# A graph attention layer on one core: TensorE adds messages up before it makes z, and two of its three signals a quad go

## Chip, cores and metric

The kernel runs on one NeuronCore of a Trainium2 chip. The metric is the device time of one execution in microseconds (us); for the kernel before it was 2990.29 us, the median of three runs (2976.26 to 2995.08).

## What is computed

Two graph layers over 6250 nodes of 128 features and 106250 edges sorted by destination, each closed by a residual and a layer norm. The change is in the attention of the second (layer 1), which the reference computes so (cut):

```python
h = _layer_norm(x, ln1_w)
xl = (h @ lin_l_w.T + lin_l_b).reshape(n, h_heads, c)     # 8 heads of 16
xr = (h @ lin_r_w.T + lin_r_b).reshape(n, h_heads, c)
e = (edge_attr @ lin_edge_w.T).reshape(-1, h_heads, c)
z = jax.nn.leaky_relu(xl[src] + xr[dst] + e, NEG_SLOPE)
logits = jnp.einsum('ehc,hc->eh', z, att)
m = jax.lax.stop_gradient(jax.ops.segment_max(logits, dst, num_segments=n))
num = jnp.exp(logits - m[dst])
den = jax.ops.segment_sum(num, dst, num_segments=n)
alpha = num / den[dst]
msg = xl[src] * alpha[..., None]
attn_out = jax.ops.segment_sum(msg, dst, num_segments=n).reshape(n, d) + attn_bias
```

Everything is float32 here but some 0/1 flags.

## The kernel before

Edges are cut into tiles of 128, four tiles are a quad (512 edges), and four quads are a group. There are 52 groups, so 208 quads. The program has three stages, one after the other: layer 0, the attention of layer 1, and the MLP with the last norm. Only the second is touched. In it each engine has its own program, written out by hand, one step for each quad Q; semaphores alone tie the engines together, and each engine takes its instructions strictly in that order.

What each engine does for a quad:

- GpSimd (POOL) issues four indirect gathers that bring the rows of `xl` of the quad's sources (L846). For quad Q it waits for z of quad Q - 4 (`z_ready`).
- SyncE (SP) loads the windows of `xr` (L830), and once a group the edge attributes and the destination offsets (L828, L826). It waits for `z_ready` too.
- TensorE (PE), `make_z`: z in PSUM is the sum of the edge attributes times a weight (L905), the window of `xr` spread over the edges by a 0/1 matrix (L909), and the gathered rows turned (L913). The last of these signals `z_ready`. `make_logits` (L925) multiplies the activated z by the attention vector and signals `lg_ready`. `add_up` (L956) multiplies the messages by a 0/1 matrix, which gives each tile's sums per destination, and signals `summed`. Once a group come `sum_ends` (L935), `spread_shares` (L940, L941) and `turn_alpha` (L948), each with a signal of its own.
- ScalarE (ACT), `split_z` (L857, L858): the leaky relu as two activations out of z's PSUM buffer, of which there are two. `keep_shrunk` (L873) takes what L941 made, once a group.
- VectorE (DVE): `make_spread` (L991) makes the 0/1 matrix for z; `add_tile` (L1022), four times a quad, adds the tile sums into the node sums in SBUF; `send_messages` (L1000) and `make_onehots` (L1010) make both operands of `add_up`; in between stand the small steps of the softmax of a group, `find_run_max` (L1042), `pick_grown` (L1146, which waits for ACT's L873), `share_out` (L1140, for which L940 waits) and others.

The order in time: in step Q, PE makes z of quad Q + 1, the logits of quad Q and the sums of quad Q - 10. DVE in its step Q makes the spread matrix of quad Q + 1, adds the sums of quad Q - 11 and makes messages and 0/1 matrices of quad Q - 9. The constant `LAG` is 9. Buffers for spread, z, messages, 0/1 matrices and tile sums are doubled.

Of the kernel before, what the change touches and what calls it, by code (L numbers as in the profile page):

```python
# [29 lines left out]
QUADS = CHUNKS // QT  # L30
# [14 lines left out]
def build(nc, t, N, E):  # L45
# [40 lines left out]
    quads = tiles // QT  # L86
# [11 lines left out]
    with ExitStack() as ctx:  # L98
# [87 lines left out]
        summed = sem("summed")  # L186
# [508 lines left out]
    attention = ExitStack()  # L695
    LAG = 9
    ROWS = 16
    AHEAD = 4
    node_sums = attention.enter_context(nc.sbuf_tensor("node_sums1", [P, NP], F32))
    with ExitStack() as ctx:  # L700
# [81 lines left out]
        z_ready = sem("z_ready")  # L782
        z_split = sem("z_split")
        lg_ready = sem("lg_ready")
# [19 lines left out]
        summed = sem("summed1")  # L804
        added = sem("added1")
        attr_dram = t["attrT"]
        with nc.Block() as block:
# [43 lines left out]
            @block.scalar  # L851
            def _(act):
                def split_z(Q):
                    act.wait_ge(z_ready, Q + 1)
                    if Q >= 2:
                        act.wait_ge(lg_ready, Q - 1)
                    nc.scalar.activation(z_act[:, Q % 2, 0, :], z_ps[Q % 2][:], ACT.Identity, bias=z_bias[:, 0:1], scale=0.2)  # L857
                    nc.scalar.activation(z_act[:, Q % 2, 1, :], z_ps[Q % 2][:], ACT.Relu, bias=z_bias[:, 1:2],  # L858
                                         scale=0.8).then_inc(z_split, 1)

                def raise_power(s):
                    act.wait_ge(lowered, s + 1)
                    nc.scalar.activation(power[:], power[:], ACT.Exp).then_inc(powered, 1)

                def raise_falls(s):
                    act.wait_ge(falls_made, 2 * s + 2)
                    nc.scalar.activation(falls[:], falls[:], ACT.Exp).then_inc(fell, 1)

                def keep_shrunk(s):
                    act.wait_ge(shares_spread, s + 1)  # L870
                    if s >= 2:
                        act.wait_ge(added, (s - 1) * CHUNKS)
                    nc.scalar.copy(shrunk[:, s % 2], shares_ps).then_inc(shrunk_made, 1)  # L873

                def norm_x1(b):
                    for i in range(block_tiles(b)):
                        at = b * QT + i
                        nc.scalar.activation(x1[:, b, i, :], x1[:, b, i, :], ACT.Identity, bias=shift1[:, at:at + 1],
                                             scale=rstd1[:, at:at + 1])

                nc.scalar.activation(std1[:], mv1[:].rearrange("p b i m -> p (b i) m")[:, :, 1], ACT.Sqrt,
                                     bias=eps_cols[:, 0:1]).then_inc(std1_made, 1)
                act.wait_ge(shift1_made, 1)
                for Q in range(quads + LAG):
                    s = Q // QUADS - 1
                    if Q < quads:
                        split_z(Q)
                    if Q % QUADS == 0 and 0 <= s - 1 < groups:
                        keep_shrunk(s - 1)
                    if Q % QUADS == 0 and 0 <= s < groups:  # L890
                        raise_power(s)
                    if Q % QUADS == 2 and 0 <= s < groups:
                        raise_falls(s)
                    if Q >= LAG and Q - LAG < blocks:
                        norm_x1(Q - LAG)

            @block.tensor
            def _(pe):
# [18 lines left out]
                def make_logits(Q):  # L917
                    s, q = Q // QUADS, Q % QUADS
                    pe.wait_ge(z_split, Q + 1)
                    if q == 0 and s >= 2:  # L920
                        pe.wait_ge(lowered, s - 1)
                    for part in range(2):
                        for i in range(QT):
                            lanes = slice(i * 32, i * 32 + 32)
                            mm = nc.tensor.matmul(lg_ps[s % 2][lanes, 0, :], att_pad[:, q, :],  # L925
                                                  z_act[:, Q % 2, part, i * P:(i + 1) * P],
                                                  start=(q == 0 and part == 0), stop=(q == QUADS - 1 and part == 1),
                                                  tile_position=(0, i * 32))
                    mm.then_inc(lg_ready, 1)

                def sum_ends(s):
                    pe.wait_ge(ends_picked, 2 * s + 2)
# [11 lines left out]
                def turn_alpha(s):  # L944
                    pe.wait_ge(alpha_made, s + 1)
                    if s:
                        pe.wait_ge(message_made, s * QUADS)
                    nc.tensor.transpose(alpha_ps, alpha[:], ident[:]).then_inc(alpha_turned, 1)  # L948

                def add_up(Q):  # L950
                    pe.wait_ge(onehot_made, Q + 1)
                    pe.wait_ge(message_made, Q + 1)
                    if Q >= 2:
                        pe.wait_ge(added, (Q - 1) * QT)
                    for i in range(QT):
                        mm = nc.tensor.matmul(tile_sums[Q % 2][:, i, :], message[:, Q % 2, i, :], onehot[:, Q % 2, i, :],  # L956
                                              start=True, stop=True)
                    mm.then_inc(summed, 1)

                pe.wait_ge(masks_made, 3)  # L960
                nc.tensor.transpose(alpha_ps[:, 0:HEADS], head_lanes[:], ident[0:HEADS, 0:HEADS])
# [7 lines left out]
                for Q in range(quads + LAG + 1):  # L969
                    s = Q // QUADS - 1  # L970
                    if Q % QUADS == 2 and 0 <= s < groups:
                        sum_ends(s)
                    if Q % QUADS == 0 and 0 <= s - 1 < groups:
                        spread_shares(s - 1)
                    if Q % QUADS == 1 and 0 <= s - 1 < groups:
                        turn_alpha(s - 1)
                    if Q + 1 < quads:
                        make_z(Q + 1)
                    if Q < quads:
                        make_logits(Q)  # L980
                    if Q >= LAG + 1:
                        add_up(Q - LAG - 1)

            @block.vector
            def _(dve):
                def make_spread(Q):
                    s, at = Q // QUADS, Q % QUADS * QW
                    dve.wait_ge(rel_in[s % 2], (s // 2 + 1) * DMA)
                    if Q >= 2:
                        dve.wait_ge(z_ready, Q - 1)  # L990
                    nc.vector.tensor_scalar(spread[:, Q % 2, :], rel_bc[:, s % 2, at:at + QW], iota_col[:, 0:1], None,  # L991
                                            ALU.is_equal).then_inc(spread_made, 1)

                def send_messages(Q):
                    s, q = Q // QUADS, Q % QUADS
                    dve.wait_ge(alpha_turned, s + 1)
                    if Q >= 2:
                        dve.wait_ge(summed, Q - 1)
                    mine = alpha_ps.rearrange("p (k l) -> p k l", k=QT)[:, :, q * HEADS:(q + 1) * HEADS]
                    nc.vector.tensor_tensor(message[:, Q % 2].rearrange("p k (h c) -> p k h c", h=HEADS),  # L1000
                                            rows[:, Q % ROWS].rearrange("p k (h c) -> p k h c", h=HEADS),
                                            mine.unsqueeze(3).to_broadcast([P, QT, HEADS, HC]),
                                            ALU.mult).then_inc(message_made, 1)

                def make_onehots(Q):
                    if Q >= 2:
                        dve.wait_ge(summed, Q - 1)
                    for i in range(QT):
                        tile = Q * QT + i
                        o = nc.vector.tensor_scalar(onehot[:, Q % 2, i, :], iota_row[:], rel_cols[:, tile:tile + 1], None,  # L1010
                                                    ALU.is_equal)
                    o.then_inc(onehot_made, 1)

                def add_tile(Q, i, base):
                    tile = Q * QT + i
                    if i == 0:
                        dve.wait_ge(summed, Q + 1)
                        dve.wait_ge(shrunk_made, Q // QUADS + 1)
                    if tile:
                        dve.wait_ge(added, tile)  # L1020
                    span = node_sums[:, bass.ds(base, P)]
                    nc.vector.scalar_tensor_tensor(span, span, shrunk[:, Q // QUADS % 2, 1, tile % CHUNKS:tile % CHUNKS + 1],  # L1022
                                                   tile_sums[Q % 2][:, i, :], ALU.mult, ALU.add).then_inc(added, 1)
# [13 lines left out]
                                            ALU.mult).then_inc(fences_made, 1)  # L1037

                def find_run_max(s):
                    dve.wait_ge(lg_ready, (s + 1) * QUADS)  # L1040
                    dve.wait_ge(fences_made, s + 1)
                    nc.vector.tensor_tensor_scan(run_max[:], fence[:, s % 2, 0:P], lg_ps[s % 2][:, 0, :], -BIG, ALU.add,  # L1042
                                                 ALU.max).then_inc(segment_step, 1)
# [156 lines left out]
                for Q in range(quads + LAG + 2):  # L1200
                    s, q = Q // QUADS - 1, Q % QUADS
# [334 lines left out]
```

## Time and profile before

| | |
|---|---|
| median of three runs | 2990.29 us |
| the profiled execution | 2994.84 us, of which 2993.0 us are the span from the first to the last instruction |
| attention of layer 1 within the span | from about 1472 to 2870 us, 208 quads |
| TensorE granted clock over the span | 0.826 of full |
| busy over the span | PE 74%, DVE 57%, ACT 38%, POOL 58% |

Times below are from that one profiled execution. PE is TensorE's matmul row, PEld its weight loads. A bracket at a row's end says how long the engine stood idle ahead of it and which instruction's signal ended that; "remote" there means a semaphore's event that the reader of the trace could not tie to one instruction that had just ended, and "issue" that nothing in the profile explains the idle time.

### The profile page before, as it was taken

Reading aid. Unit: us, or ns where it says so; the run is one execution under the profiler, and the core shown is the slowest. Engines: PE = TensorE matmul, PEld = TensorE weight load, DVE = VectorE, ACT = ScalarE, POOL = GpSimd, SP = SyncE. Lnnn points to the kernel's source line nnn. Section 1 sums busy time; section 2 is a strip of 40 time slices with the busy share of each in tenths; the row PEclk is TensorE's granted clock in tenths of the full one; section 3 lists DMA queues with packets and bytes.
Section 4 is the critical chain, followed back from the end, with each engine's and each line's share of the span. In section 5 each row is a group of like instructions: output and inputs, shape, how many; then the busy total and the mean of one; then the engine's idle time right before and its main releaser. Section 6 shows DMA issues by size and latency. Waiting matters only on the chain. (4 is left out here: it accounts for less than half of the span.)

```text
span 2993.0 us, 52671 instructions
## 1 busy us (share of the span) xinstructions
PE 2201.2 (74%) x14461; PEld 1756.5 (59%) x14461; DVE 1718.3 (57%) x7092; ACT 1126.6 (38%) x2973; POOL 1725.0 (58%) x1739
## 2 busy tenths in 40 slices
PE   7766665666666666667578888887888887888779
PEld 5665665665555666556355555555555665656556
DVE  2355555555555555557346656666666666666766
ACT  2355555555555555555333222222222222222123
POOL 3356666666666666655565656666666666666322
PEclk9687788788788877887788888987888888888879
DMA  5344444444444444432644444444444444444201
GB/s 136 97 117 111 109 112 105 113 113 109 109 111 114 106 112 112 123 88 59 171 148 141 147 142 126 144 143 140 144 146 147 144 131 139 146 146 147 62 20 36
DMA packets 378501, 356.41 MB, mean 119 GB/s; under 512 B 61695, under 2 KB 335743, under 8 KB 371424
## 3 DMA queue, kind: packets, MB, share of 16 engines
q1 hardware_dynamic: 314640, 236.51, 28.3%
q0 software_dynamic: 53248, 109.16, 14.2%
q10 hardware_dynamic: 10320, 7.37, 0.9%
q8 instruction: 118, 1.93, 0.3%
q14 instruction: 175, 1.43, 0.2%
HBM read 338.98 MB, written 13.82 MB: 118 GB/s over the span
## 5 line engine op out<-in xcount | busy, mean ns | idle before, releaser
L846 POOL DMA_INDIRECT rows<-xl_tab,src_cols x832 | 844.0, 1014 | 505.9 <-issue 228.1
L279 POOL DMA_INDIRECT rows<-in_x,src_cols x832 | 796.6, 957 | 537.0 <-issue 208.9
L330 PE MATMUL tile_sums<-gather,rows 128*128 128x128 f32 x1664 | 420.1, 342 | 254.4 <-DVE node_sums L560 172.4
L560 DVE TENSOR_TENSOR node_sums<-node_sums,tile_sums 128x256 f32 x832 | 350.0, 421 | 387.1 <-PE tile_sums L332 182.9
L330 PEld LDWEIGHTS tile_sums<-gather,rows 128*128 128x128 f32 x1664 | 322.9, 241 | 296.7 <-issue 190.1
L320 PE MATMUL p_dst<-window,spread 128*128 128x129 f32 x1664 | 331.1, 333 | 200.9 <-issue 154.1
L1022 DVE SCALAR_TENSOR_TENSOR node_sums<-node_sums,shrunk,tile_sums 128x128 f32 x832 | 280.7, 337 | 238.2 <-remote 175.6
L320 PEld LDWEIGHTS p_dst<-window,spread 128*128 128x128 f32 x1664 | 283.6, 241 | 219.8 <-issue 207.6
L332 PE MATMUL tile_sums<-gather,ones 128*128 128x128 f32 x1664 | 389.8, 323 | 0.0
L548 DVE CUSTOM_DVE_ANT_0 product<-rows,p_dst 128x128 f32<-128x128 f32 x832 | 258.2, 348 | 226.3 <-remote 147.7
L909 PEld LDWEIGHTS z_ps<-spread,window 128*128 128x128 f32 x1664 | 254.6, 221 | 155.2 <-issue 132.9
L446 ACT ACTIVATE gather<-apart,weight,minus 128x128 f32<-128x128 bf16 x832 | 342.6, 482 | 7.0 <-issue 0.2
L332 PEld LDWEIGHTS tile_sums<-gather,ones 128*128 128x128 f32 x1664 | 322.3, 241 | 0.0
L956 PE MATMUL tile_sums<-onehot,message 128*128 128x128 f32 x1664 | 297.8, 327 | 30.7 <-issue 22.5
L857 ACT ACTIVATE z_act<-z_ps,z_bias 128x512 f32<-128x512 f32 x208 | 141.8, 682 | 456.0 <-remote 218.9
L925 PE MATMUL lg_ps<-z_act,att_pad 128*32 128x128 f32 x3328 | 212.3, 299 | 121.6 <-issue 117.4
L956 PEld LDWEIGHTS tile_sums<-onehot,message 128*128 128x128 f32 x1664 | 247.1, 225 | 88.2 <-issue 75.2
L905 PE MATMUL z_ps<-attr,w_e 128*128 128x512 f32 x416 | 272.5, 740 | 12.7 <-issue 12.3
L909 PE MATMUL z_ps<-spread,window 128*128 128x128 f32 x1664 | 262.0, 307 | 13.8 <-issue 11.4
L432 ACT ACTIVATE apart<-iota_row,rel_cols 128x128 bf16<-128x128 f32 x832 | 265.7, 390 | 10.3 <-issue 3.6
L438 ACT ACTIVATE weight<-clipped 128x4 f32<-128x4 f32 x208 | 42.5, 204 | 518.1 <-issue 390.1
L925 PEld LDWEIGHTS lg_ps<-z_act,att_pad 128*32 128x32 f32 x3328 | 104.2, 115 | 208.8 <-issue 202.8
(187 smaller groups left out, 2525.7 us busy)
## 6 DMA issues: line engine op xcount, KB each, us to landing
window<-p_tab SPq DMA_DIRECT2D x832, 64.5 KB
attr<-in_attrT SPq DMA_DIRECT2D x52, 1024.0 KB
window<-xr_tab SPq DMA_DIRECT2D x832, 64.0 KB
rel_bc<-rel_rows SPq DMA_DIRECT2D x208, 128.0 KB
rel_bc<-rel_rows SPq DMA_DIRECT2D x52, 512.0 KB
rows<-in_x,src_cols POOLq DMA_INDIRECT x832
rows<-xl_tab,src_cols POOLq DMA_INDIRECT x832
p_tab<-p_rows ACTq DMA_DIRECT2D x13, 258.0 KB, 3.5
```

The costliest lines, as they stand in the source:

```text
L279: nc.gpsimd.indirect_dma_start(out=rows[:, r, i, :], out_offset=None, in_=t["x"], in_offset=bass.IndirectOffsetOnAxis(ap=src_cols[:, tile: ...
L320: mm = nc.tensor.matmul(p_dst[k][:, i, 0:P + 1], spread[:, Q % 2, at:at + P], window[:, Q % SLOTS, 2 * k + i, :], start=True, stop=True)
L330: nc.tensor.matmul(tile_sums[k][:, i, 0, :], rows[:, Q % AHEAD0, 2 * k + i, :], gather1[:, Q % 2, 2 * k + i, :], start=True, stop=True)
L332: mm = nc.tensor.matmul(tile_sums[k][:, i, 1, :], ones[:], gather1[:, Q % 2, 2 * k + i, :], start=True, stop=True)
L446: o = nc.scalar.activation(gather1[:, Q % 2, i, :], apart[:, i, :], ACT.Relu, bias=weight[:, Q % 2, i:i + 1], scale=minus[:, Q % 2, i:i + 1])
L560: nc.vector.tensor_tensor(span, span, tile_sums[i // 2][:, i % 2, :, :], ALU.add).then_inc(added, 1)
L846: nc.gpsimd.indirect_dma_start(out=rows[:, r, i, :], out_offset=None, in_=xl_tab, in_offset=bass.IndirectOffsetOnAxis(ap=src_cols[:, tile: ...
L905: nc.tensor.matmul(z[:], w_e[:], attr[:, s % 2, at:at + QW], start=True, stop=False)
L909: nc.tensor.matmul(z[:, i * P:(i + 1) * P], window[:, w, i, :], spread[:, Q % 2, i * P:(i + 1) * P], start=False, stop=False)
L925: mm = nc.tensor.matmul(lg_ps[s % 2][lanes, 0, :], att_pad[:, q, :], z_act[:, Q % 2, part, i * P:(i + 1) * P], start=(q == 0 and part == 0 ...
L956: mm = nc.tensor.matmul(tile_sums[Q % 2][:, i, :], message[:, Q % 2, i, :], onehot[:, Q % 2, i, :], start=True, stop=True)
L1022: nc.vector.scalar_tensor_tensor(span, span, shrunk[:, Q // QUADS % 2, 1, tile % CHUNKS:tile % CHUNKS + 1], tile_sums[Q % 2][:, i, :], ALU ...
```

## The change

PE's `add_up` is moved from the end of a step to a place ahead of `make_z`, so that the sums of quad Q - 10 are done before z of quad Q + 1 and not after it. Since PE's matmuls end in order, whoever sees z of quad Q + 11 then knows that the sums of quad Q are there: `wait_sums` waits for `z_ready` to reach Q + 12 and not for `summed` to reach Q + 1. `summed` is signalled for the last 11 quads alone, which no later z covers. `lg_ready` is signalled once a group, where `find_run_max` needs it, and ACT's wait for it goes, as z of quad Q comes behind the logits of quad Q - 2 in PE's order. No matmul, load or vector operation is added or taken away.

```diff
@@
     ROWS = 16
+    UNCOVERED = quads - LAG - 2
@@ split_z
                     act.wait_ge(z_ready, Q + 1)
-                    if Q >= 2:
-                        act.wait_ge(lg_ready, Q - 1)
@@ make_logits
-                    mm.then_inc(lg_ready, 1)
+                    if q == QUADS - 1:
+                        mm.then_inc(lg_ready, 1)
@@ add_up
-                    mm.then_inc(summed, 1)
+                    if Q >= UNCOVERED:
+                        mm.then_inc(summed, 1)
@@ PE's step
+                    if Q >= LAG + 1:
+                        add_up(Q - LAG - 1)
                     if Q + 1 < quads:
                         make_z(Q + 1)
                     if Q < quads:
                         make_logits(Q)
-                    if Q >= LAG + 1:
-                        add_up(Q - LAG - 1)
@@ DVE
+                def wait_sums(Q):
+                    if Q < UNCOVERED:
+                        dve.wait_ge(z_ready, Q + LAG + 3)
+                    else:
+                        dve.wait_ge(summed, Q - UNCOVERED + 1)
@@ send_messages and make_onehots, each
                     if Q >= 2:
-                        dve.wait_ge(summed, Q - 1)
+                        wait_sums(Q - 2)
@@ add_tile
                     if i == 0:
-                        dve.wait_ge(summed, Q + 1)
+                        wait_sums(Q)
@@ find_run_max
-                    dve.wait_ge(lg_ready, (s + 1) * QUADS)
+                    dve.wait_ge(lg_ready, s + 1)
```

PE's queue in the step of a group in which `sum_ends` stands (Q % 4 = 2), before. The names ahead of the arrow are what is written, and the brackets hold the semaphores waited for:

```order
L935 MATMUL ends_ps<-ends,lane_head 8x64 [waits shrunk_made,ends_picked]
L905 MATMUL z_ps<-attr,w_e 128x512 [waits z_split,attr_in1]
L909 MATMUL z_ps<-spread,window 128x128 [waits window_in1_3,spread_made1]
L909 MATMUL z_ps<-spread,window 128x128 x3
L913 MATMUL z_ps<-ident,rows 128x128 [waits gathered1_3]
L913 MATMUL z_ps<-ident,rows 128x128 x3
L925 MATMUL lg_ps<-z_act,att_pad 32x128 [waits z_split]
L925 MATMUL lg_ps<-z_act,att_pad 32x128 x7
L956 MATMUL tile_sums_0<-onehot,message 128x128 [waits added1,message_made,onehot_made1]
L956 MATMUL tile_sums_0<-onehot,message 128x128 x3
```

The same step now (`make_z` and `make_logits` stand one line higher in the file):

```order
L935 MATMUL ends_ps<-ends,lane_head 8x64 [waits shrunk_made,ends_picked]
L956 MATMUL tile_sums_0<-onehot,message 128x128 [waits added1,message_made,onehot_made1]
L956 MATMUL tile_sums_0<-onehot,message 128x128 x3
L904 MATMUL z_ps<-attr,w_e 128x512 [waits z_split,attr_in1]
L908 MATMUL z_ps<-spread,window 128x128 [waits window_in1_3,spread_made1]
L908 MATMUL z_ps<-spread,window 128x128 x3
L912 MATMUL z_ps<-ident,rows 128x128 [waits gathered1_3]
L912 MATMUL z_ps<-ident,rows 128x128 x3
L924 MATMUL lg_ps<-z_act,att_pad 32x128 [waits z_split]
L924 MATMUL lg_ps<-z_act,att_pad 32x128 x7
```

The sums into `tile_sums_0` went from behind the logits to ahead of z, and behind the group's small matmul; with them, the wait for DVE's messages now stands ahead of z.

DVE's queue over the end of one step and the start of the next (Q % 4 = 0 and 1), before:

```order
L1000 TENSOR_TENSOR message<-rows,alpha_ps 128x512 [waits summed1,alpha_turned]
L1010 TENSOR_SCALAR onehot<-iota_row,rel_cols 128x128 [waits summed1]
L1010 TENSOR_SCALAR onehot<-iota_row,rel_cols 128x128 x3
L79 TENSOR_LOAD first_row
L991 TENSOR_SCALAR spread<-rel_bc,iota_col 128x512 [waits z_ready,rel_bc_in0]
L1066 SCALAR_TENSOR_TENSOR run_sum<-inner,power 128x128 [waits powered]
L1022 ISA [waits added1,shrunk_made,summed1]
L1022 SCALAR_TENSOR_TENSOR node_sums<-node_sums,shrunk,tile_sums_0 128x128
```

And now:

```order
L1008 TENSOR_TENSOR message<-rows,alpha_ps 128x512 [waits z_ready,alpha_turned]
L1018 TENSOR_SCALAR onehot<-iota_row,rel_cols 128x128 [waits z_ready]
L1018 TENSOR_SCALAR onehot<-iota_row,rel_cols 128x128 x3
L79 TENSOR_LOAD first_row
L992 TENSOR_SCALAR spread<-rel_bc,iota_col 128x512 [waits z_ready,rel_bc_in0]
L1074 SCALAR_TENSOR_TENSOR run_sum<-inner,power 128x128 [waits powered]
L1030 ISA [waits added1,shrunk_made,z_ready]
L1030 SCALAR_TENSOR_TENSOR node_sums<-node_sums,shrunk,tile_sums_0 128x128
```

The order on DVE stays; `summed1` has become `z_ready` in three waits.

## Rows read from the trace of the kernel before

**Rows 1.** Attention of layer 1: stretch, its us, busy PE, PEld, DVE, ACT, POOL, PEclk, DMA share

```profile
1472.00:2870.00 1398.00, 1133.05 (x8268) 808.66 (x8268) 869.54 (x3430) 316.95 (x624) 830.07 (x819) 0.84 0.46 136
```

**Rows 2.** Timeline of PE, one step of layer 1 in which nothing waits

```profile
1954.12 1.02 PE L905 MATMUL z_ps<-attr,w_e 128*128 128x512 f32 x2
1954.98 1.05 PE L909 MATMUL z_ps<-spread,window 128*128 128x128 f32 x8
1955.87 0.60 PE L913 MATMUL z_ps<-ident,rows 128*128 128x128 f32 x4
1956.40 0.65 PE L925 MATMUL lg_ps<-z_act,att_pad 128*32 128x128 f32 x16
1956.97 1.16 PE L956 MATMUL tile_sums<-onehot,message 128*128 128x128 f32 x8
1958.06 0.28 PE L935 MATMUL ends_ps<-ends,lane_head 128*8 128x64 f32 x2
```

**Rows 3.** Waits of POOL, 1540 to 2800 us: total us, times, longest

```profile
POOL rows L846 <- issue: 211.8, 643, 2.0
POOL rows L846 <- remote: 161.2, 79, 2.7
POOL rows L846 <- PE z_ps L913: 83.7, 37, 3.8
POOL rows L846 <- DVE message L1000: 20.3, 12, 2.4
```

**Rows 4.** DMA issues by line, 1540 to 2800 us

```profile
rows<-xl_tab,src_cols POOLq DMA_INDIRECT x771
```

**Rows 5.** Waits of DVE, 1540 to 2800 us

```profile
DVE node_sums L1022 <- remote: 169.8, 33, 9.0
DVE picked L1146 <- ACT shrunk L873: 150.0, 34, 8.7
DVE picked L1146 <- issue: 81.7, 14, 7.6
DVE node_sums L1022 <- PE tile_sums L956: 37.6, 35, 2.7
```

**Rows 6.** Timeline around one stall of PE, all engines

```profile
1936.73 0.60 PE L913 MATMUL z_ps<-ident,rows 128*128 128x128 f32 x4
...
1937.83 1.16 PE L956 MATMUL tile_sums<-onehot,message 128*128 128x128 f32 x8
...
1938.49 0.66 ACT L857 ACTIVATE z_act<-z_ps,z_bias 128x512 f32<-128x512 f32 x1
...
1938.83 0.86 DVE L1010 TENSOR_SCALAR onehot<-iota_row,rel_cols 128x128 f32<-128x128 f32 x4
...
1941.13 0.60 PE L913 MATMUL z_ps<-ident,rows 128*128 128x128 f32 x4
...
1942.66 0.27 PE L925 MATMUL lg_ps<-z_act,att_pad 128*32 128x128 f32 x1 [0.93 <-issue]
...
1944.36 0.35 DVE L1022 SCALAR_TENSOR_TENSOR node_sums<-node_sums,shrunk,tile_sums 128x128 f32 x1 [4.18 <-remote]
...
1946.92 0.85 DVE L1010 TENSOR_SCALAR onehot<-iota_row,rel_cols 128x128 f32<-128x128 f32 x4
...
1947.80 0.47 DVE L991 TENSOR_SCALAR spread<-rel_bc,iota_col 128x512 f32<-128x512 bf16 x1
1947.92 0.29 PEld L940 LDWEIGHTS ends_ps<-shares,head_lanes 8*128 8x128 f32 x2 [2.27 <-DVE shares L1140]
```

**Rows 7.** Timeline of POOL and PE around it, to the next z

```profile
1932.49 0.96 POOL L846 DMA_INDIRECT rows<-xl_tab,src_cols  x1 [2.43 <-remote]
...
1945.12 0.96 POOL L846 DMA_INDIRECT rows<-xl_tab,src_cols  x1 [2.19 <-remote]
...
1951.17 1.06 PE L913 MATMUL z_ps<-ident,rows 128*128 128x128 f32 x4
...
1952.98 1.12 POOL L846 DMA_INDIRECT rows<-xl_tab,src_cols  x1 [2.54 <-PE z_ps L913]
```

More of the change, by code:

```diff
@@ L1006, in make_onehots @@
                     if Q >= 2:
-                        dve.wait_ge(summed, Q - 1)
+                        wait_sums(Q - 2)
                     for i in range(QT):
```

## The prediction

> **What bounds the kernel now.** I first read the busy times by stage: the attention of layer 1 takes 1398 of the 2993 us span, and no engine fills it [rows 1]. PE is the fullest at 81% (1133.05 of 1398), DVE 62%, POOL 59%. Then I asked what a step costs each engine when nothing waits. PE: from L905 at 1954.12 to the end of the sums' slot at 1958.06 [rows 2], 3.94 us a quad. POOL: a gather takes 0.96 us [rows 7] and a gap of 0.33 follows (211.8 / 643) [rows 3], so four take about 5.1 us; the quad from 1945.12 ended at 1950.44 (1952.98 - 2.54) [rows 7]. DVE: 869.54 / 208 = 4.2 us busy a quad [rows 1]. What a quad really takes: 771 gathers in the 1260 us of the steady part are 192.75 quads [rows 4], so 6.54 us. So POOL, the slowest, has about 1.2 to 1.4 us of idle time a quad, and it waits for z, which PE makes in 4 us. Something between them goes slowly.
>
> The list of POOL's waits puts the number to it: 161.2 + 83.7 + 20.3 = 265 us in 128 waits, 2.07 us each, beside the 0.3 that follows each gather in any case [rows 3]. 192.75 quads have 128 waits: so POOL often runs two quads' gathers without a pause (from 1932.49 to 1945.12 - 2.19 = 1942.93 are 10.44 us, two quads) and then stands [rows 7].
>
> The timeline tells why [rows 6]. PE's sums end at 1938.99 (1937.83 + 1.16), and DVE, which waits for them, starts at 1944.36, after 4.18 us of idle time that ended "remote". z of the next quad ends at 1941.73. PE stands for no reason that the profile gives, starting a matmul of the logits at 1942.66, and goes on at full speed from about 1944. Then DVE, ACT and POOL (1945.12) all start. So **PE's signals arrive late, several at once**, while POOL is gathering: the signal of 1938.99 took 5.4 us, where z's of 1937.33 had been there for ACT by 1938.49 at the latest. A fair part of DVE's idle time is of this kind: 169.8 + 37.6 = 207 us before the first add of a quad [rows 5]. The other part, 150.0 + 81.7 = 232 us, stands at L1146, once a group: DVE waits for ACT's L873, and this for PE's L941. Why signals are late no row says; I take the lateness as found.
>
> **The change part by part.**
>
> *Signals.* PE signals z 208 times, logits 208, sums 208. After it, logits 52 and sums 11 (208 - 197): 353 fewer. The direct cost of one: in an undisturbed step the next matmul group follows in 0.57 us after the logits' start and 1.09 after the sums' [rows 2], with no visible gap for the signal. I take 0, bounds 0 to 0.1 us each, so 0 to 35 us less. The Trainium skill ("TensorE: Matmul & The Clock Gate", The cost: per-tile semaphore tail) gives 26.3 ns for an increment on a matmul: that would be an estimated 353 x 0.026 = 9 us, and the kernel would come out inside the noise. The trace shows one signal late by 5.4 us and not by tens of ns, so the rule speaks of another situation than the stalls.
>
> *DVE's wait for the sums.* What DVE waits for before the adds of quad Q was the signal that came third after z (z, logits, sums); it is now z's own, of the same PE step. In the example: at 1939.7 DVE was done with its step (1938.83 + 0.86), and the z it would wait for is that of 1937.33, known by 1938.49. It would go on at once, and not at 1944.36. Its step, 3.4 us from the first add to the end of L1010 (1944.36 to 1946.92 + 0.85) [rows 6], would lie under the stall, and so would the spread matrix (L991 at 1947.80), on which the next z hangs. The next z ended at 1952.23 [rows 7]. It would come about 4 us sooner, at 1948.2, and POOL, done with its quad at 1950.44, would go on without the idle 2.54 us [rows 7].
>
> *What that is worth.* Not 4 us: POOL needs 5.1 us a quad, and the very next z is then signalled while POOL runs a second quad, where signals get stuck, until POOL stands again. So I expect that the runs of one quad become runs of two, and that each pair still ends in a wait. Now 128 waits; then 192.75 / 2 = 96. 32 waits fewer x (2.07 - 0.30, since the gap after a gather stays) = 57 us in the 1260 us, and x 208 / 192.75 = **61 us** in the stage. The bound above: all POOL waits go, 128 x 1.77 x 1.08 = 245 us. The bound below: none goes, 0; and less than nothing by the third rival. I take 61, as the pause after a pair is the row that I have, and nothing says it goes.
>
> *What is late next* is DVE's L1146 (232 us now). It stands at the head of the group's first step and needs PE's L941, whose signal can be stuck as before; so can those of L948 and L935, for which L1000 and L1090 wait. In the example L941 is issued in the next step, so that DVE would wait there. This is why I don't put down the 207 us of DVE's waits.
>
> *add_up ahead of z.* Same matmuls in the same ring (sums, z, logits), so PE's work is equal. But the messages of quad Q - 10 must be there 0.86 + 0.89 + 0.53 + 0.57 = 2.85 us earlier [rows 2], ahead of z and not behind the logits. What DVE's step has: before, from the end of the sums (the end of a step) to the next but one, 3.94 + 2.85 = 6.8 us; now, from z's end over the logits and one step to the sums, 0.57 + 3.94 = 4.5 us. DVE needs 3.4 us of them, plus the handovers. It holds with 1 us to spare, so 0. The group's L940, L941 and L948 now come ahead of the sums, by 1.09 us, which favours ACT's L873; but while PE waits for DVE's L1140 (2.27 us) it can no longer do the sums in the meantime: +1.09 against -1.09, 0.
>
> *ACT's second wait, DVE's third.* One wait less in 206 of ACT's instructions; ACT is busy 23% of the stage [rows 1], hidden by its idle time: 0. L1042's wait is for the same logits.
>
> *PE's clock.* It was granted 0.84 in this stage [rows 1], so a third of the time at the lower level, 1.2 GHz. If stalls shorten, this rises a little; PE isn't the bound: 0.
>
> Sum: 2994.84 - 61 = 2934 against the profiled execution. That lies 4.5 above the median of the runs, so **2930 us**.
>
> **The rivals.**
>
> A, the forecast, pairs with one pause: 2930. For it speaks the example; its own range reaches from half the gain to one and a half, 2900 to 2960. Chance 0.35.
>
> B, **fewer signals also get through better**: if lateness comes with the number that is queued (three a quad before), halving them shortens the pauses that A leaves too. Half of the rest, (245 - 61) / 2 = 92: 2838. Against it: z's own signal of 1941.73 was as stuck as the others. Chance 0.24.
>
> C, **nothing moves**: the wait at L1146 takes all that L1022 gives back. 34 + 14 = 48 waits in the 48 groups of the steady part, 4.8 us each [rows 5], speak for it; DVE would be found standing there for 232 + 207 us. The Trainium skill's price for a signal, above, would end here too. 2990, from 2960 to 3010. Chance 0.27.
>
> D, **slower**: `add_up` ahead of z puts the sums, 1.09 us, into the path from DVE to z. It decides from the point where DVE's step takes more than the 4.5 us that are left, or where DVE and not POOL sets the pace (4.2 us busy of it, with waits behind). If it does in one step of each group, and z and POOL's next gathers are late by as much: 52 x 1.09 = 57 us, 3047. Against it: DVE's 3.4 us. Chance 0.14.
>
> That the change doesn't do what it says is no rival: the queues show the order and the waits as described.
>
> **How the numbers follow.** A measurement of this kernel tells about 1%, 30 us, from no change. Faster by more than that: A for the most part (0.35), B (0.24) and a small part of C: 0.60. Within 1%: the rest of C and a part of D: 0.27. Slower: 0.13. The range: B's middle is 2838, and half of its chance reaches lower, to 2745; with 2815 below and 3015 above, about 0.1 is left out at each end.
>
> **What the changed profile would show.** Step by step: POOL's waits in the steady part, about 96 for 193 quads and 2 us each (A), or much shorter (B), or 128 again (C). DVE's wait ahead of the first add falls from 207 us to well under 100; the wait at L1146 (then eight lines lower) stays near 232 us in A and grows to about 400 in C. PE's standing within the logits gets rarer, since fewer signals are queued behind each other. In D, PE stands ahead of the sums for DVE's 0/1 matrices, and the z that follows is late. The prediction is wrong if a late signal is caused by the signals' own number and not by POOL's runs, which makes B the case, or if z's signal, which now carries everything, is itself always the late one, which makes C the case.

## The result, and the profile after

The changed kernel takes 3019.6 us (median of 11 runs, 3012.04 to 3035.7), the one before 2995.05 (11 runs): ratio 1.010, 95% interval 1.008 to 1.0121. Forecast were 2930 and a range of 2815 to 3015. The change is 1% slower where 2% faster was expected. A second comparison gave 1.012 (1.0085 to 1.0155).

The stretch 1540 to 2800 us of the changed kernel, first POOL's waits and gathers, against [rows 3, 4]:

```profile
POOL rows L847 <- remote: 160.6, 76, 2.6
POOL rows L847 <- PE z_ps L912: 125.9, 52, 5.0
POOL rows L847 <- DVE message L1008: 12.3, 5, 2.8
```

```profile
rows<-xl_tab,src_cols POOLq DMA_INDIRECT x755
```

755 gathers are 188.75 quads, 6.68 us each where before had 6.54: 0.14 x 208 = 29 us, about the loss (24.6 us between the medians). POOL's waits are 133 (0.70 a quad, before 0.66) of 2.25 us (before 2.07).

DVE's waits, against [rows 5]. L1030 is the first add of a quad, L1154 the wait for ACT's copy of shares, L1098 the carry of the maxima, which needs PE's L935:

```profile
DVE maxima L1098 <- remote: 185.1, 29, 7.4
DVE picked L1154 <- ACT shrunk L872: 181.3, 46, 8.6
DVE node_sums L1030 <- remote: 34.1, 35, 1.9
DVE message L1008 <- remote: 22.4, 8, 4.4
DVE node_sums L1030 <- PE z_ps L912: 16.1, 20, 2.0
```

The wait for the sums fell from 207 us to 50 + 7 (a row of 6.8 us more ended "issue"). In its place stand 185 us at L1098, where before had under 1 us, and 22 at L1008. L1154 has 190 us with its 8.9 of "issue" (before 232). In all, DVE waited 441 us before and 456 now.

PE, ahead of the sums:

```profile
PE tile_sums L956 <- DVE onehot L1018: 53.7, 39, 2.8
PE tile_sums L956 <- issue: 26.3, 34, 2.6
PE tile_sums L956 <- DVE message L1008: 8.7, 5, 1.9
```

Before, only 22.5 us of PE's idle time stood ahead of L956, and none of it ended with DVE. The timeline of one stall, to compare with [rows 6, 7]:

```profile
1932.27 0.28 PE L935 MATMUL ends_ps<-ends,lane_head 128*8 128x64 f32 x2
...
1934.05 0.25 DVE L1030 SCALAR_TENSOR_TENSOR node_sums<-node_sums,shrunk,tile_sums 128x128 f32 x1
...
1937.32 0.42 PE L912 MATMUL z_ps<-ident,rows 128*128 128x128 f32 x2 [0.45 <-issue]
...
1940.22 0.23 DVE L1098 TENSOR_TENSOR_SCAN maxima<-bars,maxima,ends_ps 8x16 f32<-8x16 f32 x1 [5.92 <-remote]
...
1942.54 1.41 POOL L847 DMA_INDIRECT rows<-xl_tab,src_cols  x1 [2.52 <-remote]
1942.57 0.86 DVE L1018 TENSOR_SCALAR onehot<-iota_row,rel_cols 128x128 f32<-128x128 f32 x4
...
1943.48 2.07 PE L956 MATMUL tile_sums<-onehot,message 128*128 128x128 f32 x8 [1.18 <-DVE onehot L1018]
...
1945.34 1.91 PE L904 MATMUL z_ps<-attr,w_e 128*128 128x512 f32 x2
...
1947.05 1.75 PE L908 MATMUL z_ps<-spread,window 128*128 128x128 f32 x8
...
1948.64 0.60 PE L912 MATMUL z_ps<-ident,rows 128*128 128x128 f32 x4
```

DVE is let go early, as foreseen (1934.05, no wait), and stands one instruction later, for the signal of L935, which ended at 1932.55; DVE goes on at 1940.22. PE stands too, in the middle of z, though after L935's signal it posted none before that stand, and only z's (1937.74) before DVE went on. DVE then needs until 1943.43 for the 0/1 matrices, PE's sums wait for them, and z comes behind the sums: it ends at 1949.24, 9.0 us after the release (1940.22). Two rows of before, between those of [rows 6]:

```profile
1944.69 1.16 PE L956 MATMUL tile_sums<-onehot,message 128*128 128x128 f32 x8
...
1947.92 0.39 PE L940 MATMUL ends_ps<-shares,head_lanes 8*128 8x16 f32 x2 [2.08 <-DVE shares L1140]
```

There the sums ran while DVE did its step, and z ended 7.9 us after the release (1944.36 to 1952.23), although PE also stood 2.08 us for L1140. These are one example of each, in different steps of the group. In the changed kernel's example PE's granted clock is 0.50, the lower level, from 1942 to 1948 us, after PE's idle time (sums 2.07 us against 1.16 in [rows 2], L904 1.91 against 1.02). It fell in the example of before too (0.50 from 1950 to 1952 us, after the 2.08 us), so the lower clock by itself is not what the change brought.

### The profile page after: what moved, and what is told of

Read it like the earlier page. It is cut to its first block and busy times, and to the rows that moved or that the text cites. A ratio compares the mean times of both kernels' runs of the same rounds, so it can differ in the third digit from the quotient of the medians.

```text
span 3015.1 us, 52465 instructions
## 1 busy us (share of the span) xinstructions
PE 2173.4 (72%) x14461; PEld 1754.1 (58%) x14461; DVE 1721.0 (57%) x7092; ACT 1124.7 (37%) x2973; POOL 1714.6 (57%) x1739
## 5 line engine op out<-in xcount | busy, mean ns | idle before, releaser
L847 POOL DMA_INDIRECT rows<-xl_tab,src_cols x832 | 833.6, 1002 | 547.0 <-issue 227.6
L956 PE MATMUL tile_sums<-onehot,message 128*128 128x128 f32 x1664 | 297.9, 333 | 102.3 <-DVE onehot L1018 62.3
L956 PEld LDWEIGHTS tile_sums<-onehot,message 128*128 128x128 f32 x1664 | 252.5, 232 | 139.6 <-DVE onehot L1018 86.0
L1030 DVE SCALAR_TENSOR_TENSOR node_sums<-node_sums,shrunk,tile_sums 128x128 f32 x832 | 279.5, 336 | 78.2 <-remote 34.7
L904 PE MATMUL z_ps<-attr,w_e 128*128 128x512 f32 x416 | 264.3, 723 | 8.9 <-DMA attr<-in_attrT 8.0
L908 PE MATMUL z_ps<-spread,window 128*128 128x128 f32 x1664 | 254.1, 300 | 7.2 <-issue 6.9
```

The source lines that it names most:

```text
L847: nc.gpsimd.indirect_dma_start(out=rows[:, r, i, :], out_offset=None, in_=xl_tab, in_offset=bass.IndirectOffsetOnAxis(ap=src_cols[:, tile: ...
L908: nc.tensor.matmul(z[:, i * P:(i + 1) * P], window[:, w, i, :], spread[:, Q % 2, i * P:(i + 1) * P], start=False, stop=False)
```

## The experiments

Each ratio is against the kernel before, run beside it on the same chip. The chips differ, so times are compared within one group of runs alone. The expectations weigh up two theories of the loss: O, the order (PE stands for DVE ahead of the sums, and z stands behind them), and L, the late signals of the group's small matmuls. Later ones weigh up theories of why signals are late: P, POOL's gathers; W, SP's loads.

**One part at a time.** `e1_order_alone` moves `add_up` and keeps all signals and waits:

```diff
+                    if Q >= LAG + 1:
+                        add_up(Q - LAG - 1)
                     if Q + 1 < quads:
                         make_z(Q + 1)
                     if Q < quads:
                         make_logits(Q)
-                    if Q >= LAG + 1:
-                        add_up(Q - LAG - 1)
```

> The kernel before with add_up ahead of make_z in PE's step and nothing else: summed and lg_ready are signalled for every quad and waited for as before. Theory O (the loss comes from the order: the sums, 1.1 us or more, now stand between DVE's 0/1 matrices and the z that follows, and PE stands for DVE ahead of them): 3010 to 3030 us, PE's idle time ahead of L956 that ends with DVE's onehot about 50 us or more in 1540 to 2800 us, as in the changed kernel. Theory L (the loss comes from DVE meeting the late signal of L935 after it was let go on early by z): about 2995 us, since DVE still waits for the sums' own signal, and no wait at the carry of the maxima.

Measured 3035.04 us, 1.015 (1.0125 to 1.0174). Its DVE waits in 1540 to 2800 us:

```profile
DVE maxima L1090 <- remote: 231.7, 31, 8.1
DVE picked L1146 <- ACT shrunk L873: 181.5, 45, 10.3
DVE message L1000 <- remote: 27.6, 8, 4.9
```

So the order alone makes the whole loss (44 us here, 5 us above theory O's range), and the wait at the maxima too, which theory L had said would not be there. The sums' own signal is now posted ahead of z, and so lets DVE go at least as early as z's does. PE's wait for DVE's 0/1 matrices was 45.5 us, near theory O's 50. Both theories' marks are in this run.

`e2_logits_signals` keeps the old order and takes the logits' signals and ACT's wait:

```diff
-                    if Q >= 2:
-                        act.wait_ge(lg_ready, Q - 1)
@@
-                    mm.then_inc(lg_ready, 1)
+                    if q == QUADS - 1:
+                        mm.then_inc(lg_ready, 1)
@@
-                    dve.wait_ge(lg_ready, (s + 1) * QUADS)
+                    dve.wait_ge(lg_ready, s + 1)
```

> The kernel before, in its old order, with lg_ready signalled once a group and ACT's wait for it gone; summed stays. 156 signals fewer and 206 waits fewer. If the number of PE's signals has a part in their lateness (rival B): 2950 to 2985 us. If it has none, or only the 26 ns a signal that the Trainium skill's page TensorE: Matmul & The Clock Gate gives (156 x 0.026 = 4 us by its estimate): 2988 to 2998 us, within 0.3% of before.

Measured 2992.31, 0.9997 (0.9979 to 1.0015): no effect beyond 0.2%, and the 2950 to 2985 us of rival B did not come. The interval is 5 us to either side, so it can't tell 0 from the 4 us of the estimate.

`e3_all_signals` is the changed kernel with signals posted for every quad (cut; the counts of two waits change with them):

```diff
-                    if q == QUADS - 1:
-                        mm.then_inc(lg_ready, 1)
+                    mm.then_inc(lg_ready, 1)
@@
-                    if Q >= UNCOVERED:
-                        mm.then_inc(summed, 1)
+                    mm.then_inc(summed, 1)
```

> The changed kernel with every signal posted again (208 of the logits, 208 of the sums), while its waits stay as they are: DVE waits for z. If the number of signals costs anything, slower than the changed kernel by 0.3% or more (3030 us and up). If only order and waits matter: the changed kernel's time, 3012 to 3028 us.

Measured 3035.22, 1.0144 (1.012 to 1.0168), like e1's 3035.04: whether DVE waits for z or for the sums' signal makes no difference once the order is new. The time lies in the range that was set for signals that cost something. Beside the changed kernel's 1.010 and 1.012, measured apart from this group, dropping 353 signals may give 0.2 to 0.4%; the intervals overlap, so this is not settled.

`e4_sums_first` is the changed kernel with `add_up` ahead of the group's small matmuls:

```diff
+                    if Q >= LAG + 1:
+                        add_up(Q - LAG - 1)
                     if Q % QUADS == 2 and 0 <= s < groups:
                         sum_ends(s)
...
-                    if Q >= LAG + 1:
-                        add_up(Q - LAG - 1)
```

> The changed kernel with add_up ahead of the group's small matmuls (L935, L940 and L941, L948) too. They are then 1.1 us later, but PE has the sums to do while DVE makes the shares. Theory O with cover lost at the small matmuls: 5 to 15 us faster than the changed kernel. Theory L (the signals of L935 and L941 decide, and come 1.1 us later still): slower than the changed kernel by up to 3 x 1.1 us in each of 52 groups at most, 3020 to 3100 us.

Measured 3046.74, 1.0184 (1.016 to 1.0208), 11.5 us more than e3 in the same group. That is in theory L's range, and the 5 to 15 us that theory O expected to gain did not come: the place behind the small matmuls is not what costs.

The rows can still be asked which place goes with the loss. In 1540 to 2800 us, PE's idle time that ended with an instruction of DVE, added up over all its lines, is 26 us in the kernel before and in e2, 75 and 77 us in the two profiled executions of the changed kernel, 55 in e1, 71 in e3 and 76 in e4. DVE's wait at the carry of the maxima is 186 and 166 us in the changed kernel, 236 in e1, 103 in e3 and 80 in e4, so least in the slowest. The wait at the maxima doesn't go with the loss; PE standing for DVE is found wherever the order is new. One execution each was profiled, so this points to theory O and doesn't prove it.

**What makes PE's signals late.** `e5_few_gathers`: `for i in range(QT if Q < ROWS else 1)` around POOL's gather, and PE's wait counts to match.

> The kernel before with one gather a quad in place of four in layer 1 from the 17th quad on, so three quarters of the source rows are old ones (part of the computation is left out). POOL then works 1.3 us a quad and not 5. Theory P (PE's signals are late while POOL is gathering): PE's standing within L925 (117 us as PE, 203 us as PEld in the stage before) nearly goes, waits ended by late signals go, and the stage runs at PE's and DVE's pace of 4.2 to 4.6 us a quad: about 2500 to 2600 us. Theory W (SP's window loads or the big loads of a group make them late): the standing stays at more than half, about 6 us a quad, 2850 us or more.

Measured 2569.63 beside 2992.01. From 1540 to 2300 us:

```profile
1540.00:2300.00 760.00, 739.74 (x6899) 558.24 (x6899) 710.70 (x2867) 260.27 (x526) 206.11 (x181) 0.99 0.53 167
```

```profile
DVE picked L1148 <- ACT shrunk L873: 23.0, 43, 0.9
DVE node_sums L1024 <- remote: 8.9, 1, 8.9
...
DVE node_sums L1024 <- PE tile_sums L958: 1.1, 1, 1.1
```

181 quads in 760 us are 4.2 us each. DVE waits 35 us in all, PE's idle time ahead of the logits falls from 63.1 us in the same stretch of the kernel before to 1.8, and PE's clock is 0.99. With a quarter of the gathers the late signals are gone, but for one wait of 8.9 us. This run takes away POOL's work and the gathers' traffic together, so it does not tell which of the two matters.

`e6_few_windows` loads one window of four, `e7_few_attr` the attributes for two groups alone:

> The kernel before with one window load a quad in place of four in layer 1 from the 5th quad on (three quarters of the windows are old ones, so part of the computation is left out). Theory P: late signals as before, 2970 to 2995 us. Theory W: with 48 small DMAs a group fewer, PE's standing within L925 falls by half or more, 2800 us or less.

> The kernel before with the edge attributes and the destination offsets (1.5 MB a group) loaded for the first two groups alone (the other groups use those again, so part of the computation is changed). Theory P: 2960 to 2995 us, standing as before. Theory of the big load (its burst makes PE's signals late): the one long stall in a group goes, 5 us x 50 = 250 us less at most, 2740 to 2850 us.

Measured 2963.39 and 2979.4 beside 2992.01, so 1.0% and 0.4% less, one run each (the first is 7 us below theory P's range). PE's idle time ahead of the logits in 1540 to 2300 us is 46.1 and 58.6 us, against 63.1 before, so more than half of it stays in both. SP's traffic is not the main cause.

`e8_ahead6` and `r16_ahead3` set AHEAD to 6 and 3:

> The kernel before with AHEAD 6: POOL waits for z of quad Q - 6 and so runs up to two quads further ahead. If POOL's waits for z set the pace by themselves: fewer of them, 2900 us or less. Theory P with signals late until POOL stands: POOL's runs get longer, the stalls of PE with them, and the mean stays, 2980 to 3030 us.

> The kernel before with AHEAD 3, once more. Signals late, theory P (they get through when POOL stands): 2900 to 2985 us. If POOL's pace with its waits is what counts: 3030 us or more. Signals in time: 1.002 of before, as in the last job.

Measured 3047.27 (one run, beside 2992.01) and 3001.3, 1.0049 (1.0022 to 1.0075). The first is 17 us above theory P's range and says little about it, since with AHEAD 6 POOL meets another wait. There are 16 buffers for gathered rows (`ROWS`), so for quad Q it also waits for the messages of quad Q - 16. Its waits in 1540 to 2300 us that ended with those, in the kernel before and in e8:

```profile
POOL rows L846 <- DVE message L1000: 9.6, 6, 2.3
```

```profile
POOL rows L846 <- DVE message L1000: 116.7, 30, 5.7
```

A shorter lead doesn't make the kernel better: there theory P's 2900 to 2985 us failed, and so did the rival's 3030 or more.

**A chip without late signals.** Four kernels ran on a chip on which the kernel before took 2543.28 us (17 runs).

> The kernel before with AHEAD 3: POOL waits for z of quad Q - 3, so it has one quad less that it may run ahead, and stands sooner. Theory P (PE's signals get through when POOL stands): runs of two quads and the stalls of PE that go with them get fewer, 2900 to 2985 us. If POOL's own pace with its waits is what counts: POOL waits more for z, 3030 us or more.

Measured 2549.39, 1.002 (1.0007 to 1.0034). The ranges in us were meant for the slower chips and don't apply. Its rows from 1300 to 2300 us:

```profile
DVE node_sums L1022 <- PE tile_sums L956: 167.4, 84, 6.3
DVE picked L1146 <- ACT shrunk L873: 35.1, 46, 3.7
```

```profile
POOL rows L846 <- issue: 217.0, 710, 0.9
POOL rows L846 <- PE z_ps L913: 9.7, 32, 0.3
```

POOL's gaps are its usual 0.3 us, the longest 0.9 (749 gathers in 1000 us, 5.34 us a quad), and no wait of DVE is "remote" there. PE waits for rows to land (146.9 us, 57 times). So PE's signals are late beside gathers without a pause on the four other chips that the record names and in the first comparison, whose chip it doesn't name, and not on this one. The traces do not show what sets the chips apart.

> The kernel before with AHEAD 2. Both theories: POOL now waits for a z that is made from the rows gathered two quads before, so gather, landing, z and signal stand in one chain. 3050 us or more; should the late signals cost more than this chain, below 2990 us. PE's unexplained standing within L925 (203 us as PEld in the stage before) falls by more than half in theory P.

Measured 2681.48, 1.054 (1.051 to 1.057) on that chip. POOL's waits for z are 132.1 us there (105 times, 1300 to 2300 us), against 9.7 with AHEAD 3: with signals in time this is the cost of the chain by itself.

`e11_before_no_onehots` and `e12_after_no_onehots` leave out the later 0/1 matrices from either kernel (`if Q >= 2: return` at the head of `make_onehots`, and `onehot_made` waited for up to 2):

> The kernel before with the four 0/1 matrices of L1010 made for the first two quads alone and used for all (the sums of the later quads are therefore of wrong tiles: that part is left out). DVE's step is 0.87 us shorter. Both theories: a little faster than before, since DVE's step stands between a late signal and the next z: up to 0.87 us in each of some 100 waits, 2900 to 2990 us.

> The changed kernel with the same 0/1 matrices left out. Theory O (PE stands ahead of the sums for DVE's last piece of a step, and z stands behind): the change's loss of 30 us against its partner, the kernel before with them left out, shrinks to 10 us or less, as DVE is done 0.87 us sooner. Theory L (the late signals of L935 and L941 cost it): the loss stays at 20 to 40 us.

Measured 2490.79, 0.9783 (0.9755 to 0.981) and 2490.78, 0.9786 (0.976 to 0.9811). With signals in time the change costs nothing, in this pair. The changed kernel with its 0/1 matrices did not run on that chip, so for it this is not shown. The 52 us that both gain come from POOL, which never pauses there: from 1540 to 2300 us a gather takes 0.97 us in e11 (578.52 / 596) and 1.03 in e9, which makes the matrices (586.56 / 568). From 1300 to 2300 us that is 784 gathers against 749, 5.10 us a quad against 5.34, and 0.24 x 208 = 50 us. So POOL's gathers are shorter without DVE's 0/1 matrices. (e9 differs from the kernel before in AHEAD, which was worth 0.2%.)

**The pair again, where signals are late.** The kernel before took 2984.17 us there.

> The changed kernel as it is, once more. The last job ran on a chip on which the kernel before took 2543 us and not 2990, with none of PE's signals late and POOL never waiting in layer 1. If this job's chip is of that kind: POOL sets the pace, 5.35 us a quad, and the change is worth nothing, within 0.3% of before (the only cost that could show is at the stage's end, where no gather is left to hide it: 1 to 2 us). If it is of the kind where signals are late: 1.008 to 1.013 of before, as in the first comparison.

> The kernel before without the later 0/1 matrices (that part is left out), once more. Signals late: 2900 to 2975 us, DVE's step being 0.87 us shorter behind every late signal. Signals in time: 0.978 of before, as in the last job.

> The changed kernel without them. Signals late: theory O expects its loss against its partner to shrink from 30 us to 10 or less; theory L expects 20 to 40 us. Signals in time: no difference from its partner, as in the last job.

Measured 3023.19, 1.012 (1.0085 to 1.0155); 3011.58, 1.0089 (1.0056 to 1.0121); and 2996.68, 1.0034 (1.0013 to 1.0056). Taking 0.87 us out of each of DVE's steps made the kernel before slower by 0.9%, where 2900 to 2975 us had been expected, and the changed one faster by 0.9%. The change's loss of 39 us turned into a gain of 15. That is theory O's mark, but through a partner that itself got worse for a reason that stays open, so the test is not clean. What it does show: in the kernel before, DVE's own work is not what holds this stage where signals are late.

**Slack given back and taken away.** `r17_sums_later` has the sums ahead of z for quad Q - 11, with three buffers (its diff below is cut to the order); `r18_old_order_z_waits` is the old order with waits for z.

```diff
+                    if Q >= LAG + 2:
+                        add_up(Q - LAG - 2)
                     if Q + 1 < quads:
                         make_z(Q + 1)
                     if Q < quads:
                         make_logits(Q)
-                    if Q >= LAG + 1:
-                        add_up(Q - LAG - 1)
```

> The kernel before with add_up ahead of make_z, but for quad Q - 11 and not Q - 10, with three buffers for messages and 0/1 matrices and all signals and waits of before: sums, z and logits follow each other as in the changed kernel, and the messages have a whole step more until they are needed. Theory O, as lost slack (4.5 us for DVE's step instead of 6.8): the loss of the order alone (1.015) goes, 0.997 to 1.004 of before where signals are late. If it is the place of the sums behind the group's small matmuls or ahead of z as such: 1.010 to 1.020.

> The old order (sums at the end of a step) with the changed kernel's signals: logits once a group, sums for the last quads only, and DVE waits for z of quad Q + 12 before it adds quad Q. DVE is let go 2.3 us later than before, at z's end and not at the end of the step ahead. Theory O as lost slack: 1.010 or more of before, also without the new order; the spread matrix for the next z then comes after DVE's step, 3.4 us, which would give up to 0.9 us in each undisturbed step, 1.02 to 1.06. If slack doesn't matter: 0.996 to 1.004, by the signals saved.

Measured 2985.8 and 3035.06 beside 2951.83: 1.0109 (1.0088 to 1.013) and 1.0287 (1.0267 to 1.0307). Giving DVE a whole step back took away little of the order's 1.5%: theory O as lost slack (0.997 to 1.004) failed, and the time lies in the range for the place of the sums as such. In r17's trace DVE no longer stands at the maxima, but PE now stands for DVE at the small matmuls, with the sums and DVE's adds behind them:

```profile
PE alpha_ps L948 <- DVE message L1000: 73.1, 29, 4.4
...
PE ends_ps L940 <- DVE shares L1140: 56.8, 31, 4.7
```

Such waits, PE's for DVE, are 141 us in all. So r17 took one wait away and brought others, and leaves lost slack neither shown nor ruled out. r18 lies in the 1.02 to 1.06 that was expected for a late spread matrix, and PE stands 202 us for DVE. It shows another thing too (1540 to 2800 us):

```profile
DVE node_sums L1030 <- PE z_ps L912: 403.2, 171, 4.3
...
DVE node_sums L1030 <- remote: 20.7, 4, 8.9
```

```profile
POOL rows L847 <- PE z_ps L912: 327.4, 167, 4.3
...
POOL rows L847 <- remote: 7.4, 4, 2.4
```

POOL waits 171 times in 185.5 quads, so two quads in a row without a pause are rare, and nearly all waits end by a signal that had just been posted. PE's idle time ahead of the logits is 20.4 us (108.7 before). Where POOL pauses in nearly each quad, PE's signals are in time; the pauses then cost more than the lateness did, 2.9%.

None of these kernels that does the whole work beat the one before.

## Why the prediction was wrong, point by point

*What bounds the kernel* was right: POOL is slowest, and PE's signals arrive late while it gathers (e5, r18), on all chips but one.

*Signals at 0*, and ACT's wait at 0, were right within what was measured: e2, with 156 of the 353 gone, has 0.9997. The 0.2 to 0.4% that e3 hints at lies within the bound of 0 to 35 us. That fewer signals get through better (rival B) is refuted: e2 gained nothing, and with 353 signals fewer and one other posted, L935's was still 7.7 us late.

*DVE's wait for the sums* did what the text said: 207 us became 57.

*What that is worth* is the step that failed. It took z of the next quad to come 4 us sooner and the 128 waits of POOL to become 96, worth 61 us. There were 133 in fewer quads, and they got longer, 2.25 for 2.07 us. The saved wait of DVE did not reach z, for two reasons that the text named and put at 0.

One is the next late signal: L1098 took 185 us, in *What is late next*, where only L1146 had been given a size. It waits for the signal of L935, in the group's third step, which PE issues as soon as DVE, let go early, has made its operand; in the example that signal is then held for 7.7 us.

The other is *add_up ahead of z*, put at 0 because DVE had 1 us to spare, which was reckoned with signals in time. Behind a release, DVE's 3.2 us to the 0/1 matrices, the sums and z now follow one another, 9.0 us in the example where 7.9 stood before. e1 measures the order by itself, with both reasons in it: 1.5% of the kernel, 44 us, where I had 0.

*Rival D* had the second mechanism, for one step in each group, and 57 us; 25 and 39 us were measured. Its place, PE standing for DVE ahead of the sums, is there with 54 + 9 us against none before. *Rival C's* mark, a wait in place of the one removed, is there too, though at L1098 and not at L1146.

What stays open is how the order's 44 us divide between the sums ahead of z and DVE meeting the group's signals sooner. e1 has both marks; e4, r15 and r17 each move both. That PE's standing for DVE comes with every kernel of the new order, while the wait at the maxima is less than half of e1's in e3 and e4, speaks for the sums.

## What to carry over

A wait that ends late because the signals of an engine are held up need not be won by taking it away: here the engine let go ran on to the next signal of the same engine. Before putting a price on a wait removed, list each later wait on the same source within a step, and price the first of them. And work that is moved ahead of what another engine is waiting for can cost up to its full length after a stall, even where the undisturbed step has slack for it: reckon the slack for the step behind a stall as well. Before blaming a lead or a buffer depth for a loss, look at which wait took over (e8).

## What the runs showed of the hardware

PE's signals reached the other engines late, in the example 7.7 us after the matmul had ended, and PE itself stood, while POOL issued indirect gathers without a pause. With a quarter of the gathers (e5), or with POOL pausing in nearly each quad (r18), they were in time. On one chip they were in time although POOL never paused (e9).

The same program took 2543 us on that chip and 2952 to 2995 on the others. In the profiled executions the 208 quads take 1104 us in e9 and 1351 in the kernel before (first to last L991), 247 us of the difference. Another 196 us lie ahead of the attention (its first instruction on POOL stands at 1257 and 1453 us), in a part of the program that was not looked into here.

Less work on DVE (0.87 us a quad) made the kernel 0.9% slower on a chip with late signals and 2.2% faster on the other, where a gather took 0.97 us without DVE's 0/1 matrices and 1.03 with them.
